# Adding the experts' rows by accumulating scatters into one sum in DRAM

## What is computed

```python
h = _layernorm(x) * (1 + cb) + sb                 # 2048 tokens of 128
xn = layernorm(h) * ln_gamma + ln_beta
topv, topi = top_k(softmax(xn @ router_w), 2)     # 8 experts, 2 for each token
comb = one_hot(topi) * topv / sum(topv)
out = sum over e of comb[:, e] * (silu(clip(xn @ gate_e)) * (xn @ up_e)) @ down_e     # F = 512
out = out + (silu(clip(xn @ sgate)) * (xn @ sup)) @ sdown                             # shared, F = 128
x = x + gb * out          # gb: one gate row of 128 for each of the 2 batches
```

## Time and profile before

| | |
|---|---|
| median of 3 runs | 1148.27 us (1145.86 to 1153.28) |
| profiled execution | 1150.8 us |
| its span, first to last instruction | 1149.3 us |
| PE busy | 1036.9 us (90%) |
| DVE busy | 968.1 us (84%) |
| ACT busy | 814.9 us (71%) |
| POOL busy | 520.9 us (45%) |
| mean granted TensorE clock | 0.938 |

### The profile page before, as it was taken

One profiled execution on the slowest core, in us unless ns is written; L12 is line 12 of the kernel. 1 busy time (PEld: TensorE's weight loads), 2 busy tenths in 40 slices (PEclk: granted clock), 3 DMA queues, 4 the chain that ended last, 5 costly groups with the idle time before them and its releaser, 6 DMA issues. The chain is left out here.

```text
span 1149.3 us, 21244 instructions
## 1 busy us (share of the span) xinstructions
PE 1036.9 (90%) x7771; PEld 648.5 (56%) x7771; DVE 968.1 (84%) x1309; ACT 814.9 (71%) x1621; POOL 520.9 (45%) x487
## 2 busy tenths in 40 slices
PE   6899999999999887889999999899999984699992
PEld 4222222222222334458998984468888964488992
DVE  6899999999995676979999996989999996767774
ACT  3279898999998644978888844888888922265561
POOL 5400431010101211027899991048999972256663
PEclk9779999999999988799999999899999995699996
DMA  5210100001000420107999980118999967311124
GB/s 158 69 43 15 30 16 21 25 16 30 15 2 2 130 56 2 58 2 178 244 248 224 223 205 3 58 43 193 234 242 224 242 144 253 41 43 41 43 48 121
DMA packets 58374, 114.40 MB, mean 100 GB/s; under 512 B 15406, under 2 KB 28718, under 8 KB 58272
## 3 DMA queue, kind: packets, MB, share of 16 engines
q0 software_dynamic: 14880, 50.23, 22.2%
q1 hardware_dynamic: 40152, 60.62, 16.8%
q10 hardware_dynamic: 3240, 2.20, 0.7%
HBM read 55.47 MB, written 9.13 MB: 56 GB/s over the span
## 5 line engine op out<-in xcount | busy, mean ns | idle before, releaser
L2245 PEld LDWEIGHTS m_pair<-filter_w,delta_x_t 128*128 128x128 f32 x2560 | 294.0, 192 | 43.1 <-issue 43.1
L559 DVE TENSOR_REDUCE neg_max<-max_ps 128x1 f32<-128x1024 f32 x256 | 295.6, 1214 | 15.2 <-PE max_ps L548 15.0
L2245 PE MATMUL m_pair<-filter_w,delta_x_t 128*128 128x112 f32 (+3 forms) x2560 | 298.5, 276 | 9.8 <-DVE h_t L2272 3.3
L675 ACT ACTIVATE exp_scores<-score_k 128x512 f32<-128x512 f32 x512 | 270.8, 605 | 28.4 <-PE score_k L667 22.7
L2221 ACT ACTIVATE decay<-delta,a_log 128x1024 f32<-128x1024 f32 x128 | 145.7, 1142 | 49.7 <-DVE normed L2272 29.7
L548 PE MATMUL max_ps<-k_rows,q_rows 48*128 48x512 bf16 x512 | 163.0, 400 | 12.4 <-DVE neg_max L559 10.7
L2213 ACT ACTIVATE filter_w<-filter,b_t 128x112 f32<-128x112 f32 (+1 forms) x576 | 167.4, 374 | 0.0
L667 PE MATMUL score_k<-q_rows,k_rows 51*128 51x512 bf16 x512 | 163.0, 389 | 2.4 <-ACT exp_scores L675 0.6
L694 PE MATMUL av_ps<-exp_scores,v_cols 128*32 128x256 f32 x2048 | 158.2, 394 | 0.0
L568 POOL CAST neg_max_parts<-neg_max 128x16 bf16<-128x16 f32 x16 | 3.2, 197 | 235.0 <-DVE neg_max L559 235.0
L694 PEld LDWEIGHTS av_ps<-exp_scores,v_cols 128*32 128x32 f32 x2048 | 44.2, 109 | 92.0 <-ACT exp_scores L675 52.8
(11 more groups left out here) (335 smaller groups left out, 1631.4 us busy)
## 6 DMA issues: line engine op xcount, KB each, us to landing
c_row<-c_rows SPq DMA_DIRECT2D x64, 512.0 KB, 6.0
x_inner<-normed POOLq DMA_DIRECT2D x16, 512.0 KB, 6.5
delta_x<-mod_memory POOLq DMA_DIRECT2D x15, 512.0 KB, 8.1
delta_x<-x_inner POOLq DMA_DIRECT2D x15, 512.0 KB, 8.3
x_inner<-h_t POOLq DMA_DIRECT2D x14, 512.0 KB, 5.7
mod_memory<-h_t POOLq DMA_DIRECT2D x14, 512.0 KB, 9.2
mod_memory<-normed POOLq DMA_DIRECT2D x12, 512.0 KB, 8.8
gate_up_all<-in_gate_up_w SPq DMA_DIRECT2D x8, 512.0 KB, 7.3
```

The source lines that it names most:

```text
L559: ve.tensor_reduce(nm[leg % 2][:, 4 * j + qt:4 * j + qt + 1], mps[:, bank:bank + 2, :].rearrange("p a q -> p (a q)"), AX_X, ALU.max, negat ...
L675: ac.activation(pt[a % 4][:, HEADS[r % 4], :], eps[:, bank, :], ACT.Exp, scale=SC).then_inc(*exped.up())
L2245: mm = pe.matmul(vps[blk][:, lo:hi], self.duT[b][:, c, blk * P:(blk + 1) * P], wf[g % 3][:, lo:hi], start=True, stop=True)
```

## The change

The rows of both choices and of the shared expert are no longer kept apart. A tensor `sum_dram` ("moe_sum") begins as x plus the gated shared expert, and every tile's rows are added to it in DRAM by an indirect DMA with `compute_op=ALU.add`. In detail:

- `n_dram` rows become 257 wide: 128 normed values, the choice's weight, and the 128 gate values of the token's batch. The gate columns are written by SP after attention's last transfers (`sp_gate_rows`).
- The gate is multiplied into the shared expert's down weights (`po_gate_shared`), and into a tile's output together with the choice's weight in one operation, now on DVE (`ve_tile_out`), with four buffers.
- `dst` of a second choice is the token's row as well (one dependent operation more in `ve_rows`).
- DVE does all four hidden products of the shared expert. Its down projections stay in PSUM, and `ve_add_shared(c)` adds chunk c to X, ahead of the loop, after which SP stores it to `sum_dram`.
- `po_scatter(j)` waits until scatter j - 1 has landed (scatter 0 for the four stores of x). The output of tile j waits until scatter j - 4 has landed.
- In the loop the copy of the down weights stands before `ve_hidden`.
- Stage 3 goes. `store` waits for the last scatter and copies the 2048 rows from `sum_dram` to the output, DRAM to DRAM.

```diff
+    def sp_gate_rows(self):
+        sp = self.sp
+        sp.wait_ge(*self.m_row)
+        for i in range(2):
+            for b in range(NB):
+                lo = i * TOK + b * S
+                sp.dma_start(self.n_dram[lo:lo + S, D + 1:2 * D + 1].rearrange("(k p) d -> p k d", p=P),
+                             self.mrow[1][:, b, 5:6, :].to_broadcast([P, TB, D])).then_inc(*self.gate_put.up(16))
...
+            def po_gate_shared():
+                po.wait_ge(*self.in_moe.at())
+                for b in range(NB):
+                    po.tensor_tensor(sdn[:, b, :], self.moe_w["shared_down_w"][:], self.mrow[1][:, b, 5, :],
+                                     ALU.mult).then_inc(*shared_gated.up())
...
+                ve.tensor_scalar(other[:], row[:], float(P + TOK), -float(TOK), ALU.is_ge, ALU.mult).then_inc(*route.up())
                 ve.wait_ge(*route.at())
-                ve.scalar_tensor_tensor(out=dst[:], in0=row[:], scalar=-float(P), in1=empty[:], op0=ALU.add,
+                ve.scalar_tensor_tensor(out=row[:], in0=row[:], scalar=-float(P), in1=other[:], op0=ALU.add,
                                         op1=ALU.add).then_inc(*route.up())
+                ve.wait_ge(*route.at())
+                ve.tensor_tensor(dst[:], row[:], empty[:], ALU.add).then_inc(*route.up())
...
-            for c in (2, 3):
+            for c in range(NC):
                 ve_shared_hidden(c, ups[c])
...
-            def ac_tile_out(j):
-                ac.wait_ge(dn_mm.sem, j + 1)
-                if j >= 3:
-                    ac.wait_ge(y_put[j % 3].sem, 16 * (j // 3))
-                ac.activation(yo[j % 3][:], yps[j % 2][:, 0:D], ACT.Copy, scale=xg[j % NG][:, D:D + 1]).then_inc(*y_out.up())
+            def ve_tile_out(j):
+                ve.wait_ge(dn_mm.sem, j + 1)
+                wait_from(ve, y_put.sem, 16 * (j - NY + 1))
+                ve.scalar_tensor_tensor(out=yo[j % NY][:], in0=yps[j % 2][:, 0:D], scalar=xg[j % NG][:, D:D + 1],
+                                        in1=xg[j % NG][:, D + 1:], op0=ALU.mult, op1=ALU.mult).then_inc(*y_out.up())
...
             def po_scatter(j):
-                s = j % 3
                 po.wait_ge(y_out.sem, j + 1)
-                po.indirect_dma_start(y_dram, bass.IndirectOffsetOnAxis(dst[:, j:j + 1], 0), yo[s][:], None).then_inc(
-                    *y_put[s].up(16))
+                if j:
+                    po.wait_ge(y_put.sem, 16 * j)
+                else:
+                    po.wait_ge(*x_put.at())
+                po.indirect_dma_start(sum_dram, bass.IndirectOffsetOnAxis(dst[:, j:j + 1], 0), yo[j % NY][:], None,
+                                      compute_op=ALU.add).then_inc(*y_put.up(16))
...
+            def ve_add_shared(c):
+                added[c] = self.ve_out(self.X, c, banks[c])
+                sp_put_x(c, added[c])
...
             pe_up(0)
+            ve_add_shared(2)
+            ve_add_shared(3)
             ve_clip(0)
...
+                if j + 2 < NTILE:
+                    ve_weights_down(j + 2)
+                if j + 1 < NTILE:
                     ve_hidden(j + 1)
                 pe_down(j)
-                if j + 2 < NTILE:
-                    ve_weights_down(j + 2)
-                ac_tile_out(j)
-                if 4 <= j < 4 + NT:
-                    ve_add_shared(j - 4)
+                ve_tile_out(j)
                 po_scatter(j)
...
     def store(self):
         sp, stored = self.sp, self.sig("stored")
+        sp.wait_ge(*self.summed_rows)
+        sp.dma_start(self.out.rearrange("b (p k) d -> (b p) (k d)", p=P // NB),
+                     self.sum_dram[0:TOK].rearrange("(p k) d -> p (k d)", p=P)).then_inc(*stored.up(16))
```

More of the change, by code:

```diff
@@ L2512, in experts @@
             hd = [sb(f"hidden{s}", [P, CH]) for s in range(2)]
[L2513 to L2518, removed]
+            NY = 4
+            yo = [sb(f"tile_out{s}", [P, D]) for s in range(NY)]
+            n_dram = self.n_dram
+            sum_dram = nc.dram_tensor("moe_sum", (TOK + NTILE * P, D), F32, kind="Internal").ap()
+            (w_in, n_put, fixed, route, exp2, sh_clip, sh_silu, weigh, x_mm, x_out, w_copy, d_copy, up_mm, clip, gate,
+             hid, dn_mm, y_out, x_put, y_put, shared_gated) = (self.sig(n) for n in (
                 "experts_in", "normed_put", "route_const", "route", "exp_second_done", "shared_clip", "shared_silu",
-                "shared_hidden", "weigh", "x_mm", "x_out", "gate_up_copy", "down_copy", "gate_up_mm", "clipped", "gate_silu",
-                "hidden", "down_mm", "y_out", "mixed"))
+                "weigh", "x_mm", "x_out", "gate_up_copy", "down_copy", "gate_up_mm", "clipped", "gate_silu",
+                "hidden", "down_mm", "y_out", "x_put", "y_put", "shared_gated"))
             x_in = [self.sig(f"x_in{s}") for s in range(NG)]
-            y_in = [self.sig(f"y_in{c}") for c in range(NC)]
-            y_put = [self.sig(f"y_put{s}") for s in range(3)]
             for e in range(E):
@@ L2804, in experts @@
             logits = [ring.take(b) for b in range(NB)]
-            gates, ups = ({c: ring.take(i) for c, i in enumerate(two)} for two in ((2, 3), (5, 6)))
+            gates, ups = {c: ring.take(2 + c) for c in (0, 1)}, {}
             self.ve_neg_mean(0, TB, self.norm_root)
@@ L2963, in experts @@
             po.wait_ge(*rows_to)
-            ac_weights(0)
-            shared = [ac_shared_out(c, banks[c]) for c in range(NC)]
-            ve.wait_ge(*shared[-1])
-            for j in range(2):
-                ac_weights(j + 1)
-                pe_tile_turn(j)
-                ve_tile_turn(j)
-                ve_weights_down(j)
+            for j in range(3):
+                ac_weights(j)
+            for mark in (counted, gates[2].left):
+                pe.wait_ge(*mark)
+            pe_tile_turn(0)
+            ve_tile_turn(0)
+            pe_shared_down(2, banks[2])
+            ve_add_shared(0)
+            ve_weights_down(0)
+            pe_tile_turn(1)
+            ve_tile_turn(1)
+            pe_shared_down(3, banks[3])
+            ve_add_shared(1)
+            ve_weights_down(1)
+            for mark in (ups[2].left, slots.left):
+                pe.wait_ge(*mark)
             pe_up(0)
+            ve_add_shared(2)
+            ve_add_shared(3)
             ve_clip(0)
@@ L2975, in experts @@
             ve_hidden(0)
-            for mark in shared:
-                pe.wait_ge(*mark)
+            for c in range(NC):
+                pe.wait_ge(*added[c])
             for j in range(NTILE):
```

83 lines of the change are left out of this document (24 added, 59 removed).

## The result

The changed kernel is slower: 1187.9 us (median of 6 runs, 1179.7 to 1198.9) against 1150.8 for the kernel before beside it (6 runs, 1145.9 to 1159.3), a ratio of 1.0303 with a 95% interval of 1.0255 to 1.0351. The ratio leaves out the run of 1198.9 us, which stood over 1.5% above the fastest of its kernel. The forecast was 1138, with a range of 1129 to 1168. The profiled execution took 1187.3 us, its span is 1185.8, 36.5 longer than before.

A forecast was written before the change was run, and what follows sets the result against it. TensorE was taken to bound the late loop at 2.79 us a tile, the scatter chain after the change at 2.97: 1018.7 + 38 x 2.97 + 2.7 + 0.1 + 4.6 = 1139.0 end, so 1138 us, range 1129 to 1168.

The forecast's parts named there:

- What bounds the kernel, and the mechanism: Tile loop: TensorE paces late tiles at 2.79 us; after the change, the larger of 2.79 and L + w, forecast 2.97.
- the second rival: Scatter chain slower than today's kernel, L above 2.96 from row-by-row handling or longer issue; 1169 us at L 3.5; 35%.
- L, the time to the landing: Accumulating scatter, start to landing: 2.0 + 0.33 + 0.34 = 2.7 us; lower bound 2.2, upper open.
- w, from landing to start: Scatter chain on GpSimd: time from one landing to the next scatter's start, taken as 0.27 us.
- The floor of GpSimd: GpSimd's loop: scatter issue 0.99, gather 0.97 and gaps 0.30 and 0.27 set a least pace of 2.53 us.
- the first rival: Loop's scatters stay hidden behind TensorE, L + w below 2.79; 1131 us; chance 20%.
- Whom the late scatter stops: Loop: VectorE waits for buffer j-4 before output j, then TensorE; gathers, six tiles ahead, cost nothing.
- VectorE's part of a tile: Tile loop: VectorE's cycle becomes 2.72 us, so without the scatters TensorE paces at 2.79, returning 8.1 us.
- The start: Ahead of the loop: first down projection 1.2 us later, first output 0.5 more; first scatter at 1018.7, bounds 1017 to 1020.5.
- Gate rows: During attention: four 512 KB transfers on SP cost nothing, since SP waits for its next work anyway.
- The tail: After the last landing: 0.1 us wake and one DRAM-to-DRAM copy of 4.6 us (3.8 to 8.7); 11.3 us gained.
- The third rival: Loop: output on VectorE is the bound; at 0.5 us instead of 0.30 the cycle is 2.92; 1136 us; no chance given.

The follow-up runs named there:

- e5: Changed kernel, each accumulating scatter taking only the first 64 of a tile's 128 rows (half the rows left out of the sum): 1175.5 us, one run.
- e6: Changed kernel, each accumulating scatter sending 64 of the 128 columns of each row, to a tensor of its own: 1184.5 us, one run.
- e1: Changed kernel with plain scatters in place of accumulating ones, each still waiting for the landing ahead; adding left out: 1144.8 us, ratio 0.9897 to the kernel before.
- e2: Changed kernel with accumulating scatters to rows of their own, none waiting for the one ahead; sum of choices left out: 1147.1 us, ratio 0.9918.
- e4: Changed kernel with even and odd tiles added to two sums in DRAM, joined at the end; full result: 1155.3 us, ratio 0.9981.
- e13: e9 with the copy of the down weights behind hidden, as in the kernel before; full result: 1140.2 us, ratio 0.9898.
- e14: Kernel before with one edit, the copy of the down weights ahead of hidden; full result: 1139.8 us, ratio 0.9916.
- e3: Changed kernel with plain scatters to rows of their own and no chain; sum of choices left out: 1145.3 us, ratio 0.9902.
- e8: Changed kernel with plain unchained scatters to 4096 separate rows and a tail with two adds a chunk; full result: 1154.2 us, ratio 0.9984.
- e11: e9 with gathered rows 257 wide, their gate columns loaded and not used; full result: 1157.4 us, ratio 1.0005.
- e7: Changed kernel with a memset of one private column on GpSimd between the two waits and the scatter; same result: 1189.2 us, one run.
- e15: e9 with three output buffers instead of four; full result: 1160.3 us, ratio 0.9993.
- e18: e3 unchanged, run again beside e15: 1154.1 us, ratio 0.9930.
- e9: e8 with the output on ScalarE, gathered rows 129 wide and three operations a chunk in the tail; full result: 1155.1 us, ratio 1.0008.
- e16: e9 unchanged, run again beside e15: 1155.6 us, ratio 0.9939.

## Why the prediction was wrong

*What bounds the kernel, and the mechanism.* Right. The wait of scatter j on landing j-1 sets the pace, in all 38 links, and the second rival named it.

*L, the time to the landing.* This is the first step that failed: 2.7 forecast, 3.3 measured, 38 x 0.6 = 23 us of the miss of 46.8. The packet's price (0.33 us) was taken from accumulating packets of 4 KB, and an accumulating scatter has none of these: it has eight packets of 512 bytes an engine, 0.71 us with the semaphore's (the windows beside e5 and e6). The second term was left out altogether: GpSimd works 1.59 us on the issue and not 0.99. The rival had both as its conditions; I held it back to 35% because the 4 KB packets ran without a stop, which says nothing about rows of 512 bytes. With an L of 3.3 alone the sum would have been 1018.7 + 38 x 3.57 + 3.3 + 4.7 = 1162.4, so 1161 us, still within the range. Of the Trainium skill's page (DMA: Bandwidth & Descriptors, "Anatomy of one DMA — SWDGE (gpsimd) path") the fit of 2.0 us plus bytes over 436 GB/s, an estimate of 2.15 for 64 KB, is near the plain scatter (2.25 measured in e1) and not the accumulating one (3.3). Its line on descriptor generation, "You can emit a lot of descriptors before the incremental cost shows up", is not borne out for the accumulating scatter: 64 rows fewer shorten its issue by 0.16 us (e5).

*w, from landing to start.* 0.27 forecast, 0.75 measured (e1). I took a gap behind an engine's signal for a wait on a landing. This is the second step that failed, and I gave it no bounds at all: 38 x 0.48 = 18 us of the miss, which carried the time out of the range. With both terms right the sum would have been 1016.4 + 38 x 4.05 + 3.3 + 0.1 + 5.8 = 1179.5; the last 6 us are the nine links that landed late, 4.8 us at most. No output came late.

*The floor of GpSimd.* I put it at 2.53 us a tile; with the real issue it is 3.19 (e2, and so in e4), over TensorE's 2.79. So the first rival, hidden scatters at 1131, could not have come true even with a short L.

*Whom the late scatter stops.* I named VectorE at its output buffer; it has no wait for a landing in the record. It was TensorE, at the gather behind the waiting scatter, which I had called harmless beside the wait since it is six tiles ahead. The head start was used up 9 us behind the first scatter: TensorE waits for a gather first at 1025.8 (0.23 us) and next at 1029.9 (1.34).

*VectorE's part of a tile.* Right in size where it can be seen by itself: 106.3 and 105.5 us (e13, e14) against 106.0 by the late pace. But I counted it as sure, and with both edits and no chain it does not come (e3, e8 to e11). I also ascribed it to freeing VectorE of 16 pairs of adds and to the copy together, where the copy alone is enough (e14), and so is the rest without it (e13). The output took 0.34 us, forecast 0.30.

*The start.* The first scatter at 1016.4 lay below my bound of 1017, for the stages ahead of the loop ran 1.6 us earlier than in the record of before (the first normed rows are written at 967.4 and not at 969.0). The first down projection starts 0.9 us earlier than before, which leaves 0.7 for the term of 1.2, and from there to the scatter there are 0.3 us more for the term of 0.5. *Gate rows* cost nothing, as said. *The tail* held: one transfer, no VectorE work; 5.8 us for the copy, within 3.8 to 8.7 but 1.2 above the value taken.

*The third rival* (output on VectorE as the bound) played no part: in 1020 to 1160 us of the changed kernel VectorE waits 32 times for the gate and up products and 27 times for the transposed rows.

## What to carry to other kernels

Where each DMA waits for the landing of the one ahead, the price is the landing and what lies between it and the next start, here 3.0 us from start to start for a plain indirect scatter of 64 KB and 4.0 for an accumulating one; a chain through memory is to be compared with the stage's pace at that price, before any work that it saves. Take the price of a packet only from packets of the same size, and look for what else is in the queue of the engine that will wait. Where a profile names what an engine waited for, count the instructions before believing it. And try an edit's parts alone: here the copy moved into a wait brought some 10 us, as much as the whole change had been credited with.

## What was not expected of the hardware

- An indirect scatter with addition is one packet for each row of 512 bytes (144 packets in all), a plain one 32 packets, 16 of them of 4 KB. Its issue takes GpSimd 1.59 us for 128 rows and 1.43 for 64, against 0.99.
- GpSimd is awake 0.11 us after a landing, but the indirect instruction starts some 0.6 later (e7).
- Every link of over 4.2 us in the two records of the changed kernel, 16 in all, has a packet of an instruction queue in it; of the other 60 links 12 have one.
- With plain unchained scatters, the adds out of the loop and the copy ahead, VectorE stops with no releaser in the record, in nine records on four chips (e3, e8 to e11, e15 to e18): 6 to 11 times in a record for over 1 us from 1020 us on, and for 3.5 us at most. ScalarE stops with it, for up to 2.0 us, where the output is on ScalarE (e9, e11, e15, e16). With the copy alone (e14), or the rest without the copy (e13), there are none. What stops them stays open: the edits change the order of instructions as well as the moments at which engines meet.
